# A layer norm in four blocks: who makes the squares of blocks 1 and 3

## The reference

```
def _layernorm(x, axis=-1, eps=1e-05):
    m = jnp.mean(x, axis=axis, keepdims=True)
    v = jnp.var(x, axis=axis, keepdims=True)
    return (x - m) / jnp.sqrt(v + eps)
```

## Time and profile before

| | us |
|---|---|
| median of 3 runs | 3429.51 (3428.8 to 3432.13) |
| the profiled execution, its own time | 3426.57 |
| its span in the trace | 3424.8 |
| busy: TensorE / VectorE / ACT / POOL | 2778.6 / 1825.0 / 1380.9 / 765.7 |

### The profile page before, as it was taken

How to read it: one execution, slowest core, us unless ns; L and a number is a source line. 1 busy time by engine, 2 the same in 40 slices (tenths; PEclk the granted TensorE clock), 3 DMA queues, 4 the chain that set the end, 5 groups by cost and what they waited for, 6 DMA issues and landing times. The chain is left out here.

```text
span 3424.8 us, 57880 instructions
## 1 busy us (share of the span) xinstructions
PE 2778.6 (81%) x22862; PEld 1420.1 (41%) x22862; DVE 1825.0 (53%) x3512; ACT 1380.9 (40%) x2682; POOL 765.7 (22%) x721
## 2 busy tenths in 40 slices
PE   6665778778888768889858889899888988777986
PEld 3454336623336633334332222243233443654546
DVE  4311135369885368830178887611396454537733
ACT  3310434353224337662347777633303233234552
POOL 1000004426535420000245440000361000240003
PEclk8766778978888979999979999999799998887987
DMA  2023001212101231000040220000160001022102
GB/s 114 15 58 85 1 0 43 55 45 74 62 19 46 84 74 33 23 2 0 0 74 15 32 32 1 1 0 12 40 157 13 1 1 50 14 59 69 35 9 74
DMA packets 84405, 130.25 MB, mean 38 GB/s; under 512 B 15584, under 2 KB 52928, under 8 KB 82856
## 3 DMA queue, kind: packets, MB, share of 16 engines
q1 hardware_dynamic: 71528, 106.68, 11.4%
q0 software_dynamic: 9152, 16.71, 2.0%
q10 hardware_dynamic: 3456, 3.15, 0.3%
HBM read 99.93 MB, written 25.85 MB: 37 GB/s over the span
## 5 line engine op out<-in xcount | busy, mean ns | idle before, releaser
L1787 DVE TENSOR_REDUCE at_mp<-PS 128x1 f32<-128x384 f32 (+3 forms) x640 | 306.7, 536 | 85.0 <-PE PS L1610 72.6
L1736 ACT ACTIVATE at_pt<-PS 128x384 f32<-128x384 f32 (+3 forms) x704 | 270.3, 455 | 190.2 <-PE PS L1610 156.5
L1602 PE MATMUL PS<-at_kx,at_qx 48*128 48x384 bf16 (+5 forms) x640 | 198.6, 347 | 60.6 <-DVE at_mp L1787 21.6
L1630 PE MATMUL PS<-at_qx,at_kx 57*128 57x512 bf16 (+5 forms) x704 | 192.8, 314 | 9.7 <-ACT at_pt L1736 9.4
L4235 ACT ACTIVATE ls_pt<-PS,ls_far 128x512 f32<-128x512 f32 x256 | 155.5, 685 | 24.8 <-PE PS L4056 17.9
L4382 DVE CUSTOM_DVE_ANT_0 PS<-PS,ls_pt 128x1024 f32<-128x1024 f32 x128 | 153.9, 1239 | 19.4 <-ACT ls_pt L4235 16.5
L1610 PE MATMUL PS<-at_above,identb 64*128 64x128 bf16 (+1 forms) x1408 | 160.7, 212 | 0.0
L1610 PE MATMUL PS<-at_other,at_eye 64*128 64x128 bf16 (+1 forms) x1408 | 158.2, 208 | 0.0
L2507 DVE TENSOR_TENSOR_SCAN mb_ring<-PS,mb_ring 128x1024 f32<-128x1024 f32 x64 | 146.6, 2291 | 19.3 <-POOL mb_ring L2446 6.7
L2462 PE MATMUL PS<-mb_ring,ident 128*128 128x512 f32 x256 | 149.1, 736 | 5.9 <-DVE mb_ring L2512 5.9
L1113 DVE SCALAR_TENSOR_TENSOR X<-PS,small_L,X 128x512 f32<-128x512 f32 x8 | 6.0, 751 | 261.2 <-PE PS L1061 261.2
(11 more groups left out here) (833 smaller groups left out, 6527.2 us busy)
## 6 DMA issues: line engine op xcount, KB each, us to landing
rw_arena<-rw_v_rows SPq DMA_DIRECT2D x32, 512.0 KB, 4.6
dl_arena<-in_fir_bank SPq DMA_DIRECT2D x32, 256.0 KB, 3.1
lnA<-mb_rows SPq DMA_DIRECT2D x16, 512.0 KB, 3.6
XN<-mb_rows SPq DMA_DIRECT2D x16, 512.0 KB, 3.4
ffn_place<-in_ffn_L SPq DMA_DIRECT2D x4, 1152.0 KB, 17.1
x_rows<-mx_t SPq DMA_DIRECT2D x16, 256.0 KB, 2.4
mx_s<-y_rows SPq DMA_DIRECT2D x16, 256.0 KB, 4.7
ffn_place<-in_ffn_L SPq DMA_DIRECT2D x4, 1024.0 KB, 9.2
```

The source lines that it names most:

```text
L1602: mm = nc.tensor.matmul(PS[:, n % 3, 0:e - c], QX[rows, u % 3, g, blk(i, P)], KX[rows, u % 3, g, c:e], start=True, stop=True)
L1630: mm = nc.tensor.matmul(PS[:, 3 + n % 3, 0:e - c], KX[rows, u % 3, g, blk(j, P)], QX[rows, u % 3, g, c:e], start=True, stop=True)
L1736: nc.scalar.activation(PT[:, y % SLOTS, g, 0:e - c], PS[:, 3 + n % 3, 0:e - c], ACT.Exp, scale=SCALE).then_inc(exp_done, 1)
L1787: nc.vector.tensor_reduce(best, sc, AX.X, ALU.max).then_inc(s_maxed, 1)
```

## The change

VectorE makes the squares of blocks 1 and 3: it copies PSUM bank b to `k.XN`, waits for its own copy, and multiplies that by itself into `k.lnA`. ACT makes those of blocks 0 and 2. On VectorE both squares stand ahead of the four scalings. The scalings of blocks 1 and 3 read the copy in `k.XN` in place of the PSUM bank. ACT's order becomes square 0, root 0, square 2, root 1, root 2, root 3. TensorE's order stays; `variance(b)` waits for ACT's count in even blocks and for VectorE's in odd ones. The stage has two more semaphores.

```diff
-                pe.wait_ge(squared, b + 1)
+                pe.wait_ge(squared_here if b % 2 else squared, b // 2 + 1)
...
             square(0)
-            square(1)
-            for b in range(NBLK):
+            root(0)
+            square(2)
+            for b in range(1, NBLK):
                 root(b)
-                if b + 2 < NBLK:
-                    square(b + 2)
...
         @block.vector
         def _(dve):
+            def square(b):
+                dve.wait_ge(centered, b + 1)
+                nc.vector.tensor_copy(dst[:, blk(b)], PS[:, b, :]).then_inc(held, 1)
+                dve.wait_ge(held, b // 2 + 1)
+                nc.vector.tensor_tensor(sq[:, blk(b)], dst[:, blk(b)], dst[:, blk(b)], ALU.mult).then_inc(squared_here, 1)
+
+            def scale(b):
+                dve.wait_ge(root_done, b + 1)
+                nc.vector.tensor_tensor(dst[:, blk(b)], dst[:, blk(b)] if b % 2 else PS[:, b, :], rstd[:, blk(b)], ALU.mult).then_inc(scaled, 1)
+
+            square(1)
+            square(3)
             for b in range(NBLK):
-                dve.wait_ge(root_done, b + 1)
-                nc.vector.tensor_tensor(dst[:, blk(b)], PS[:, b, :], rstd[:, blk(b)], ALU.mult).then_inc(scaled, 1)
+                scale(b)
```

More of the change, by code:

```diff
@@ L113, in layernorm @@
     sq, rstd = k.lnA, k.lnA
-    with stage(nc, "centered", "squared", "var_ready", "log_done", "root_done", "scaled", "pool_own") as (block, centered, squared, var_ready, log_done, root_done, scaled, pool_own):
+    with stage(nc, "centered", "squared", "squared_here", "var_ready", "log_done", "root_done", "scaled", "held", "pool_own") as (block, centered, squared, squared_here, var_ready, log_done, root_done, scaled, held, pool_own):
         if beside is not None:
```

## The result

The changed kernel is slower. The median of 20 runs is 3444.27 us, that of the kernel before in the same jobs 3429.62; the ratio is 1.0034 (95% interval 1.002 to 1.0048), 11.7 us on 3429.5. Two more measurements of the same two kernels gave 1.0004 (0.9987 to 1.0021) and 1.004 (1.0022 to 1.0057). The forecast was 6.8 us. The first measurement's interval is 6.9 to 16.5 us; a mean of the three measurements, weighted by their intervals, is about 1.0027, or 9 us with some 3 to either side (an estimate). So the sign holds. That the whole is above 6.8 us is what the middle values say, and it isn't clear of the noise.

A forecast was written before the change was run, and what follows sets the result against it. Each norm stage was taken to hang on block 3's variance matmuls, and those on its square. Terms 5.5 + 0.3 + 0.9 + 0.2 gave 6.8 us unrounded, so 3436.3 us, 0.20% slower; 8-in-10 range 3431 to 3441.5.

The forecast's parts named there:

- The delay of V3: Block 3's variance matmuls start 0.425 us later, waiting for VectorE's copy and multiplication; 5.5 us over 13 norm stages.
- S3's leaving: Block 3's square leaves ACT between an exponential and block 2's logarithm; ACT's freed time can't be used, at most 1.1 us.
- M0 to M2 hide: Last multiplications of blocks 0 to 2 queue behind block 3's square on VectorE; hidden, with 0.5 us to spare.
- Block 1's square: On VectorE before block 1's variance matmuls; late by about 0.13 us each in stages at 1517 and 2799, sum 0.3.
- POOL beside it: Norms where POOL makes constants: 0.15 us at 2617, 0.1 at 2380, 0.6 where POOL ends the stage; sum 0.9.
- the sum: All terms of the forecast added over the 14 norm stages: 6.9 us, or 6.8 us with the terms unrounded.
- the bound of 0.88 for iota and memset: Block 3's square beside POOL's iota (1202) or memset (3068): priced at nothing, at most 0.88 us each.
- the rule of the Trainium skill: VectorE instructions with two SBUF inputs contend with GpSimd instructions that read SBUF, not with ones that only write.
- the rival: Clock lost in matmuls behind a norm as TensorE idles longer: 1.8 us in three stages, 5.4 more, 3441.7; chance 0.15.

The follow-up runs named there:

- e8: The changed kernel with two matmuls without use behind block 3's variance matmuls in each norm, against the kernel before: 0.9948 (0.9929 to 0.9967), median 3462.43 us.

## Why the prediction was right in its mechanism and short in its size

**The delay of V3: right.** Forecast 0.42 to 0.43 per stage, V3 2.52 behind C3; measured 2.53, and 0.43 to 0.44 in the stages at equal clock (those at 679, 2698, 2799 and 3061). The copy took 0.69, the multiplication 0.69, their starts 0.73 apart. That S3's leaving is worth nothing held as well, and that M0 to M2 hide. This was the main term, and the 14 norm stages are 7.5 longer in all where the forecast had 6.8. Part of that closeness is luck, since losses and gains of clock of up to 2.3 in single norms happened to cancel.

**Block 1's square: right in kind, too large.** In the norm at 2712 V1 was not late (C3 again 0.85 behind V1). The stage at 2799, for which I had 0.13, is 12.94 with this square on VectorE and 12.95 with block 3's alone. With block 1's square alone the one at 1517 is 12.07, between the 11.90 and 12.17 of two profiles of the kernel before. So the forecast's 0.3 us is not to be seen.

**POOL beside it: mis-sized.** I had 0.15 for the stage at 2617, 0.1 for the one at 2380 and 0.6 for the one that POOL ends. The last measured 0.84. The first, in the one profile where it kept the clock, was 11.17, against 11.12 with block 3's square alone: 0.05. In the one at 2380 the error was of another kind. I priced what the selects do to the square and left out what the four VectorE operations do to the selects there, because POOL wasn't the one that ended the stage in the profile I read. It becomes that one, and at full clock it already was. With a clock of 0.88 and 0.89 and the two idle matmuls the stage is 14.02 in the kernel before, 14.45 with one input from PSUM and 15.09 in the changed kernel: 0.43 for the delay and 0.64 for POOL. At a clock near 1.00 it is 13.95 before, 13.91 with one input from PSUM and 15.60 after: the delay hides behind POOL, and POOL costs 1.7. The two stages together cost 1.9 to 2.5 where the sum had 1.1 (0.6, 0.1 and 0.43).

In the changed kernel's first profile every square beside an iota or a memset alone took 0.69; the only longer ones are the one of 1.04 and one of 0.79, both beside selects. Its other profiles have up to three longer squares each, of 0.80 to 1.05, one of them of 0.90 in the stage at 2617 for which the forecast had a wait. So the bound of 0.88 for iota and memset was not used. On this point too the rule of the Trainium skill (SBUF — State Buffer, Who interferes with whom) agrees with the runs.

**The clock: the rival is seen in some stages, and its size stays open.** I gave 0.15 to stages losing the clock behind a norm, 1.8 us each, with three such stages at stake. One of the three lost it in every profile: the first layer 1 stage was 152.59 in two profiles of the kernel before and 155.30 to 155.32 in three of the changed one. Layer 2's second was 69.02 and 69.03 against 70.72 to 71.85. Together these two are 5.1 us on the average. In the first of them the first eight matmuls took 973 ns on the average where the next eight took 592, in the changed kernel (groups of the stage's first 25 us, count, busy us, mean ns, idle):

```profile
L1043 PE MATMUL PS<-XN,ffn_place 128*128 128x512 f32 x8 | 6.4, 973 | 2.5 <-PEq L77 2.5
L1051 PE MATMUL PS<-XN,ffn_place 128*128 128x512 f32 x8 | 3.6, 592 | 0.0
```

and in the kernel before they took 601:

```profile
L1033 PE MATMUL PS<-XN,ffn_place 128*128 128x512 f32 x8 | 3.7, 601 | 2.5 <-PEq L77 2.5
```

My argument against the rival was that the idle time of 2.53 behind V3 was longer already and unchanged. It did not protect this stage: TensorE's idle time before V3 grew from 0.21 to 0.65, and the stage that had kept its clock lost it. It kept it, at 152.6, in both profiles of the kernel before and with block 1's square alone. Of seven profiles with V3 late and no idle matmuls it lost it in six (154.3 to 155.7). The seventh is the one with the longest delay, where TensorE was idle for 0.94 before V3:

```profile
1539.81:1692.40 152.59, 151.30 (x352) 1.00 0.00 0
```

So more idle time before V3 is not enough by itself, and what else decides is not shown. With TensorE kept at work behind V3, and V3 as late as ever, both stages are back (e8).

The clock also went the other way: the norm at 2964 ran at 0.76 before (13.38) and at 1.00 after (11.13), and the stage at 2394 took 77.5 and 78.2 before and 75.1 to 76.0 after. The first four matmuls of the seven stages, where I had priced the rival, took 19.1 to 21.3 us in the changed kernel against 19.8 and 20.8: no clear loss. Some of these gains and losses repeat in every profile of a kernel, such as the ones named so far. Others differ between profiles of one kernel: layer 1's second stage was 152.59 and 154.29 in the kernel before, the norm at 2617 was 12.62, 11.17 and 12.55 in the changed one. So that the 5.1 us of two chosen stages is about what the first ratio has above the sum (4.9) is no proof that they are its cause.

**What stays open.** The attention stage at 3097 is 226 us in two profiles of before and 233.7, 227.0 and 233.6 in three of after, with a granted clock of 0.92 or 0.93, and of 0.88, 0.92 and 0.88. It begins 25 us behind the norm, and these runs don't tie it to it. Nor do they say how much of the ratio each stage holds, or whether there is a rest above the sum at all: single executions of one kernel spread over 20 us.

## What to carry to other kernels

Taking work off an engine pays only if the helper has the result ready sooner where somebody waits for it. Here V3 waited for the square of block 3. The helper needed two operations (1.51 us from C3's end to V3) where ACT, late as it came, had V3 start after 1.08. What ACT gained was time in front of its logarithms, where it waited for TensorE. When an added instruction reads two tiles in SBUF, look for POOL work beside it and ask in both directions who waits, and whether POOL then ends the stage. And where TensorE idles before a barrier, try a few matmuls without use: here they were worth 0.5%, more than the edit under study cost.

## What the runs showed that I had not expected

Two matmuls without use in each of 14 norms, behind V3, made the program 18 us faster (0.9947 and 0.9948 in two jobs), with the norms themselves no shorter. And a delay of 0.72 us in 13 stages cost 16.8 us, 1.8 times its own sum, though the interval reaches down to 9.6, next to the sum's 9.4.
